# Expert tiles of the third feed-forward: on the load queue the store of a tile's outputs is issued two loads later

## The reference, cut to what matters

```
disp = zeros((E, cap, D)).at[e_flat, p_flat].add(x_rep * kmask[:, None])
h = gelu(einsum('ecd,edh->ech', disp, w1) + b1[:, None, :], approximate=False)
y = einsum('ech,ehd->ecd', h, w2) + b2[:, None, :]
yk = y[e_flat, p_flat]
out = (yk * w[:, None]).reshape(N, K, D).sum(axis=1)
```

## Time and profile before

| | us |
|---|---|
| median of 3 runs | 4508.24 (4508.11 to 4510.07) |
| profiled execution, its own time | 4515.06 |
| span of the profiled execution | 4513.3 |
| PE busy | 3588.2 (80%) |
| DVE busy | 3366.9 (75%) |
| ACT busy | 2318.5 (51%) |
| POOL busy | 1558.9 (35%) |
| mean granted TensorE clock | 0.876 |

### The profile page before, as it was taken

How to read it: one execution, slowest core, us unless ns; L and a number is a source line. 1 busy time by engine, 2 the same in 40 slices (tenths; PEclk the granted TensorE clock), 3 DMA queues, 4 the chain that set the end, 5 groups by cost and what they waited for, 6 DMA issues and landing times. The chain is left out here.

```text
span 4513.3 us, 95409 instructions
## 1 busy us (share of the span) xinstructions
PE 3588.2 (80%) x31831; PEld 2498.6 (55%) x31831; DVE 3366.9 (75%) x6253; ACT 2318.5 (51%) x4148; POOL 1558.9 (35%) x906
## 2 busy tenths in 40 slices
PE   4984979996897999930477505999869999699999
PEld 2553646665564666630355303666546666577777
DVE  5888879997897888860244325888877878688888
ACT  2432657773674666610233203677656666366665
POOL 1210045550002555427200265555244544122222
PEclk9985989996898999955678756999979999699999
DMA  4000022221001222111111112222221211200000
GB/s 131 15 28 23 0 64 64 64 62 54 1 0 42 58 60 56 43 43 52 47 42 47 46 47 59 61 57 61 65 48 45 55 46 44 72 15 14 14 14 14
DMA packets 161161, 200.26 MB, mean 44 GB/s; under 512 B 37948, under 2 KB 109952, under 8 KB 159809
## 3 DMA queue, kind: packets, MB, share of 16 engines
q1 hardware_dynamic: 152769, 180.75, 14.9%
q0 software_dynamic: 8192, 16.79, 1.3%
HBM read 52.96 MB, written 33.55 MB: 19 GB/s over the span
## 5 line engine op out<-in xcount | busy, mean ns | idle before, releaser
L709 ACT ACTIVATE a_p<-a_p 128x480 f32<-128x480 f32 x832 | 501.6, 603 | 517.2 <-DVE a_p L557 514.8
L353 POOL TENSOR_TENSOR a_km<-a_k,a_slots 96x1920 fp32r<-96x1920 f32 x186 | 631.7, 3415 | 179.5 <-DMA a_k<-a_kh 179.5
L552 DVE TENSOR_REDUCE a_mx<-a_sc 128x4 f32<-128x480 f32 (+1 forms) x832 | 542.4, 652 | 128.4 <-PE a_sc L797 98.9
L557 DVE TENSOR_TENSOR a_p<-a_sc,a_mx 128x480 f32<-128x480 f32 x832 | 531.3, 639 | 18.8
L715 ACT ACTIVATE a_pt<-a_tp 120x512 f32<-120x512 f32 x832 | 487.7, 586 | 84.3 <-PE a_tp L806 79.1
L806 PE MATMUL a_tp<-ident,a_p 128*120 128x128 f32 x3328 | 511.0, 276 | 4.1 <-ACT a_p L709 2.3
L806 PEld LDWEIGHTS a_tp<-ident,a_p 128*120 128x120 f32 x3328 | 401.2, 138 | 89.9 <-ACT a_p L709 27.1
L791 PE MATMUL a_sc<-a_km,a_qr 96*128 96x480 f32 x768 | 396.2, 516 | 33.4 <-DMA a_qr<-a_ql 29.3
L830 PE MATMUL a_nd<-a_pt,a_vm 120*32 120x128 f32 x6656 | 354.8, 285 | 0.0
L830 PE MATMUL a_nd<-a_pt,a_dm 120*32 120x128 f32 x6656 | 334.6, 273 | 0.0
L763 PE MATMUL a_pj<-a_ctx,a_wk 128*128 128x480 f32 x128 | 73.1, 655 | 251.8 <-DMA a_ctx<-in_ctxT 251.8
(11 more groups left out here) (426 smaller groups left out, 9124.8 us busy)
## 6 DMA issues: line engine op xcount, KB each, us to landing
a_qr<-a_qh SPq DMA_DIRECT2D x384, 64.0 KB, 2.0
a_k<-a_kh SPq DMA_DIRECT2D x384, 60.0 KB, 2.0
a_ctx<-in_ctxT SPq DMA_DIRECT2D x64, 240.0 KB, 2.7
a_qr<-a_ql SPq DMA_DIRECT2D x192, 64.0 KB, 2.0
a_k<-a_kl SPq DMA_DIRECT2D x192, 60.0 KB, 2.0
dispatched<-zero SPq DMA_DIRECT2D x8, 1024.0 KB, 10.2
f_xr<-dispatched SPq DMA_DIRECT2D x32, 256.0 KB, 2.8
expert_rows<-f_yo SPq DMA_DIRECT2D x32, 256.0 KB, 2.0
```

The lines of the kernel that those rows point to most:

```text
L353: v.tensor_tensor(KM[par][:, i, :, :].rearrange("p b (j k) -> p b j k", k=KN), K3[:, i, :, :].unsqueeze(2).to_broadcast([TR, GB, 4, KN]), ...
L552: v.tensor_reduce(mx[:], view, AX.X, ALU.max).then_inc(mx_ready, 1)
L557: v.tensor_tensor(PR[s % 4][:].rearrange("p (h k) -> p h k", k=k), view, mx[:].unsqueeze(2).to_broadcast([P, heads, k]), ALU.subtract).the ...
L709: a.activation(PR[s % 4][:], PR[s % 4][:], ACT.Exp).then_inc(exp_ready, 1)
```

## The change

The loop on SP runs two steps longer, and in step t it issues the load of tile t + 2 (as before) and then the store of tile t - 2, in place of the store of tile t. The semaphore value and the tile number of the store go back by two as well; the buffer index t % 2 is the same for both. No wait is added or taken away, no other engine's instructions change.

```
-                for t in range(NT):
+                for t in range(NT + 2):
                     if t + 2 < NT:
                         load(t + 2)
-                    sp.wait_ge(Z["yo_ready"], t + 1)
-                    sp.dma_start(tile_of(R.expert_rows, t), YO[t % 2][:]).then_inc(stored[t % 2], 16)
+                    if t >= 2:
+                        sp.wait_ge(Z["yo_ready"], t - 1)
+                        sp.dma_start(tile_of(R.expert_rows, t - 2), YO[t % 2][:]).then_inc(stored[t % 2], 16)
```

## The result

The changed kernel takes 4364.26 us, the median of 4 runs (4362.95 to 4366.73), against 4509.15 for the kernel before (4508.11 to 4514.88). The ratio is 0.9676, with a 95% interval of 0.9662 to 0.969. The forecast was 4362, range 4350 to 4390. Its profiled execution took 4362.95 us, with a span of 4361.2.

A forecast was written before the change was run, and what follows sets the result against it. The expert part was held by PE's wait for f_xr loads queued behind stores waiting for f_yo. Load wait 84.6 and clock 62 us make 146.6; 4508.24 - 146.6 = 4361.6, rounded to 4362, range 4350 to 4390.

The forecast's parts named there:

- The bound: Expert part: PE waits 29 times for the load of f_xr, 84.6 us, placed behind a store waiting for f_yo.
- The sum: Whole kernel: median 4508.24 less 146.6 us gained in the expert part gives 4361.6, in round figures 4362.
- The whole-tile measure: Expert part, tiles 2 to 31: 29 tiles of 11.90 us become 6.84 each, as tile 1; gain 146.6 us.
- Its two terms: Expert part: the load wait of 84.6 us goes whole, and the clock, taken as 1.00, decides 62 us.
- What was costed at nothing: Expert part: 32 stores moved behind later loads cost nothing, hidden by ten us of other work.
- the spare time: Stores on SP: late only if landing some 13 us, nearly two tiles, after issue; they land within 3.0 us.
- The long issue of a load: Loads on SP: issue has taken up to 1.53 us; about 7.8 us are to spare before the load is read.
- The first rival: Expert part: wait goes, f_xl's short wait keeps the clock low; only 84.6 us gained, 4423.6; chance 0.05 in full.
- The signs to look for: Expert part: f_xr wait under 3 us, load 0.8 behind store, tiles 6.8 apart, clock above 0.98, last f_yo about 2410.6.
- What would be late next: First matmul of each tile: PE waits 0.27 us for f_xl; without it the gain is 7.8 us more.
- the shortest tile: Expert part: a tile without the wait for f_xl takes 6.57 us, in place of 6.84.

The follow-up runs named there:

- one load of lead: Changed kernel with the store issued one load later in place of two: 4347.27 us, ratio 0.9677 to the kernel before.
- The filled wait: Kernel before with 12 needless matmuls of 512 columns in PE's wait for the load of tiles 3 to 31: 4454.35 us, ratio 0.9922.
- six-matmul kernel: Kernel before with 6 needless matmuls in PE's wait for the load of tiles 3 to 31: 4407.32 us, ratio 0.9808.
- the earlier f_xl: Changed kernel with DVE's split of f_xl one unit earlier, behind the second unit of a tile: 4336.09 us, ratio 0.9648.

## Why the prediction was right

- **The bound.** That the expert part was held by the load's place behind the store, and there by the store's wait for f_yo, is shown three ways: PE's wait goes with the change, it goes with one load of lead as well, and it comes back when the load waits for f_yo in the new order.
- **The sum.** 146.6 us were forecast, and 146.6 are missing between the first and the last f_yo. The whole-tile measure was right to 0.01 us: the 29 tiles from 2202.41 to 2400.75 take 6.84 each. The profiled executions differ by 4515.06 - 4362.95 = 152.1; the other 5.5 lie mostly between the gather and the last feed-forward, which the change doesn't touch. The medians differ by 144.9, 1.7 less than forecast, and the median before is 4509.15 with the fourth run, 0.9 above the 4508.24 of the forecast. Together that is the 2 us by which 4362 was missed. That it is so little is in part luck: between the two profiled executions untouched phases moved by as much (the gather from 173.0 to 175.0, the attentions from 566.8 to 563.4 and from 620.4 to 617.3).
- **Its two terms.** 84.6 for the wait and 62.0 for the clock. The 62.0 is what is left of the 146.6, 2.14 us for each of the 29 tiles; the clock shown behind a wait is 0.52 over 3.44 us, and PE is busy for 61.9 us less after the change. The filled wait gave back 57.9 in the part with the load as late as ever. The clock was therefore some two fifths of the gain, and what brings the clock down is PE's idle time, not the late load as such. That price was read off the tiles of this very wait; 25 waits of nearly the same length with five loads cost some 20.6 us of clock, 0.8 each and not 2.14.
- **What was costed at nothing.** The later place of the store did cost nothing, up to four loads, and the spare time was well counted: the store has to land nearly two tiles late to hold ACT. The long issue of a load came again (1.43 us once) and was hidden.
- **The first rival.** The granted clock is 1.00 over 207.6 us, with f_xl's pause of 0.35 us in every tile. Pauses of this length did not bring it down here.
- **The signs to look for.** All came: no wait for f_xr, tiles 6.84 apart, the load 0.86 us behind the store, the last f_yo at 2409.92 (2410.6 forecast), the gather 3.40 us after it.
- **A term too small.** What would be late next was f_xl, priced at 7.8 us; taken away it was worth 10.4 in the part, since its pause is 0.35 and not 0.27 us. The 6.84 us of the forecast holds the pause either way, so the sum didn't suffer; only the shortest tile, 6.57, should have been 6.49.

## What to carry to other kernels

On a queue that issues loads and stores, a store's wait for the end of a tile must not be the last thing ahead of the load that the next tile needs (here it cost 84.6 us of wait and 62.0 of low clock); write the order so that each load waits only for its own buffer, and count how many tiles of delay the store's buffers bear (here four loads later cost nothing and five cost 96.4 us). Price a wait of PE by the whole tile against one that had no wait, since the work behind the wait may run at a lower clock (0.52 over 3.44 us here), and don't carry that price over to another wait of the same length (2.14 us a tile here, 0.8 with five loads). When an edit adds or removes instructions on PE, compare the phases that it doesn't touch (one took 620 or 585 us here) before its total is believed.

## What the runs showed of the hardware

- Idle PE of 2.83 us was followed by 3.44 us at a granted clock of 0.52. The waits of 1.3 to 1.6 us in the six-matmul kernel were not, nor the pauses of 0.35 us in the changed kernel. In between the length alone doesn't tell. Counting a granted clock below 1.00 in the 3.44 us behind a wait, low clock followed 27 of 29 waits before (2.7 to 3.7 us), 10 of 25 with the store five loads later (2.6 to 3.3 us), 19 of 29 where the load waits for f_yo (2.4 to 3.0 us) and 2 of the 9 longer ones in the six-matmul kernel (2.1 to 2.7 us).
- A loop of attention that wasn't edited takes 620 or 585 us (66 or 13 packets on the queue named "q8 instruction"), by what stands ahead of it in PE's code. 174 needless matmuls, hidden in a wait, make the whole kernel some 34 us faster, with the earlier f_xl (4336.09 to 4301.65) as without. It is the second largest gain of this study.
- The same kernel differs by 15 to 17 us between the first chip and three others, and the gather of 128 indirect DMAs (173.0 against some 158.7 us) holds nearly all of it.
